# Clustered linear layer: count, gates and bias reordered, and the first value products of attention issued around the count

## The chip, the cores and the metric

The kernel runs on one NeuronCore of a Trainium2 chip. The metric is the device time of one execution in microseconds (us); a kernel's time is the median of several executions. Engines are called PE (TensorE), DVE (VectorE), ACT (ScalarE), POOL (GpSimd) and SP (SyncE).

## The reference, cut to what matters

Two layers over x of 16 x 64 tokens by 512 features. Layer 0 is a channel attention and then the clustered linear layer; layer 1 is a cross-attention with 32 query and 8 key/value heads, and a quantised SwiGLU. The change lies in the clustered linear layer and at the start of layer 1's attention.

```python
x = x + tanh(g_xattn[0]) * channel_attention(layernorm(x), ctx)
# clustered linear, on h = layernorm(x)
dots = softmax(h @ centroids.T / 0.1)          # 64 clusters
hits = dots > 0.01
query_sel = any(hits, axis=1)                  # per token
cluster_sel = any(hits, axis=0)                # per cluster, over ALL tokens
row_sel = cluster_sel[assignments]             # per output feature
dense = h @ weight.T + bias
x = x + tanh(g_ffn[0]) * where(query_sel[:, None] & row_sel[None, :], dense, 0)
# attention of layer 1 (masked softmax with rope), keys and values from ctx
k, v = ctx @ wk, ctx @ wv ;  q = layernorm(x) @ wq
x = x + tanh(g_xattn[1]) * attention(q, k, v) @ wo
x = x + tanh(g_ffn[1]) * swiglu_quantised(layernorm(x))
```

No token's output can be gated before the hits of all 1024 tokens are known, since `cluster_sel` runs over all of them.

## The kernel before, in words

Tokens lie in 8 tiles of 128 partitions (`TILES`), features in 4 chunks of 128 (`KC`). Each engine has its own program, and the programs are kept together by semaphores (`then_inc`, `wait_ge`). The order on each engine is written by hand. A large matmul is three matmuls of rounded parts: a high part `_hi` (made by ACT) and a rest `_lo` (made by DVE or POOL).

**`clustered_linear`** does this for tile `t`, with `p = t % 2` naming the buffers:
- DVE normalises `x_sb` into `xn` (`normalize`, two tiles ahead of the transposes' products); PE transposes it into the PSUM bank `TP[p]`; ACT rounds it (`split`, line 541) and DVE takes the rest (`split`, line 575).
- PE makes 24 matmuls (`products`, lines 660 and 662) into `DA[p]` (64 cluster columns and 224 dense ones) and `DB[p]` (288 dense ones). Tile t's products need the bank of tile t-2 free, so PE waits for that tile's exponential and its two bias additions (`s_exp`, `s_dense`).
- DVE takes the row maximum and scales it (lines 580, 583), adds the bias to both halves (585, 587), ACT takes the exponential (547). ACT's exponential also waits for the first bias addition, `act.wait_ge(s_dense, 2 * t + 1)`, and ACT's `split(t + 2)` stands behind the exponential.
- DVE (`hit`) inverts the sum, thresholds (594), adds the hits into `hit_sum` (597), takes the row's maximum (599) and multiplies by the gate (603).

After tile 7, PE multiplies `hit_sum` by ones into `CNT` (682), DVE turns the count into `selected` (636), and PE multiplies it by the one-hot assignments into the bank `ROW` (686). Then the block ends, and all engines meet before the next one.

**Weight pieces.** `raw` is a ring of 4 buffers. Eleven pieces (`NEXT`) of the first attention weights are loaded ahead; ACT rounds a piece (`round_piece`, 763) and POOL takes the rest (`split_piece`, 771), which counts in `s_piece`. Places 0 to 3 (two pieces of `wv`, two of `wq`) are rounded ahead of tile 0's exponential. Places 4 to 6 (`RING` to `FIRST`) are rounded by ACT behind the loop over tiles 0 to 5, ahead of the exponentials of tiles 6 and 7.

**`attention_and_swiglu`** begins in the next block. PE makes the value products of tiles 0 to 4 (12 matmuls of 256 columns each; `FIRST_V[t]` is half of the double bank `PB2`), with `key(0)` (12 matmuls of 512) in front of tile 2. DVE goes through `gate_linear(t)` (line 1484: dense times row gate times `ROW`), the row statistics of the updated rows (`rows`, behind POOL's `add_linear`), the rests of the values (`rest_v`, line 1432, behind ACT's rounding), and then normalises the tiles (`normalize_x`, line 1493), which PE transposes ahead of the first queries. From there on come ropes, scores and outputs.

Of the kernel before, what the change touches and what calls it, by code (L numbers as in the profile page):

```python
# [21 lines left out]
F32 = mybir.dt.float32  # L22
# [7 lines left out]
P = 128  # L30
# [444 lines left out]

def clustered_linear(nc, d, c):
# [12 lines left out]
    with ExitStack() as ctx:  # L489
# [20 lines left out]
        row_hit = sb("row_hit", [P, 2])  # L510
# [3 lines left out]
        TP = [bank("TP0_"), bank("TP1_")]  # L514
# [22 lines left out]
        @block.scalar  # L537
        def _(act):
            def split(t, p):
                act.wait_ge(s_t, t + 1)  # L540
                nc.scalar.activation(xt_hi[:, p, :, :], TP[p][:, :].rearrange("p (k t) -> p k t", k=KC),
                                     ACT.Copy).then_inc(s_hi, 1)

            def softmax(t, p):
                act.wait_ge(s_maxt, t + 1)
                act.wait_ge(s_dense, 2 * t + 1)
                nc.scalar.activation(e_cl[:, p, :], DA[p][:, 0:CLUSTERS], ACT.Exp,
                                     bias=nmax_t[:, p:p + 1], scale=INV_TEMPERATURE,
                                     accum_out=zsum[:, p:p + 1]).then_inc(s_exp, 1)

            split(0, 0)
            split(1, 1)
            for place in range(RING):
                round_piece(nc, act, c, 0, place, 0, *NEXT[place][:2])
            with act.Fori(0, TILES // 2 - 1) as i:
                for p in range(2):
                    softmax(2 * i + p, p)
                    split(2 * i + p + 2, p)
            for place in range(RING, FIRST):
                round_piece(nc, act, c, 0, place, 0, *NEXT[place][:2])  # L560
            for p in range(2):
                softmax(TILES - 2 + p, p)

        @block.vector
        def _(dve):
# [12 lines left out]
            def softmax_and_bias(t, p):  # L578
# [4 lines left out]
                nc.vector.tensor_scalar(nmax_t[:, p:p + 1], nmax[:, p:p + 1], INV_TEMPERATURE, None,  # L583
                                        ALU.mult).then_inc(s_maxt, 1)
                nc.vector.tensor_tensor(dense[:, t, 0:DENSE_A], DA[p][:, CLUSTERS:HALF],
                                        bias[:, 0:DENSE_A], ALU.add).then_inc(s_dense, 1)
                nc.vector.tensor_tensor(dense[:, t, DENSE_A:D], DB[p][:, 0:HALF],
                                        bias[:, DENSE_A:D], ALU.add).then_inc(s_dense, 1)

            def hit(t, p):  # L590
# [5 lines left out]
                dve.wait_ge(s_hit, t + 1)  # L596
                nc.vector.tensor_tensor(hit_sum[:, :], hit_sum[:, :], hits[:, p, :], ALU.add)\
                  .then_inc(s_sum, 1)
                nc.vector.tensor_reduce(row_hit[:, p:p + 1], hits[:, p, :], AX.X, ALU.max)\
                  .then_inc(s_row, 1)  # L600
                dve.wait_ge(s_row, t + 1)
                dve.wait_ge(s_sum, t + 1)
                nc.vector.tensor_tensor(row_gate[:, t, :], row_hit[:, p:p + 1], tg[:, 2:3], ALU.mult)\
                  .then_inc(s_gate, 1)
# [14 lines left out]
            def tile(t, p, ahead):  # L619
                softmax_and_bias(t, p)  # L620
# [3 lines left out]
                hit(t, p)  # L624

# [6 lines left out]
            for p in range(2):  # L632
                softmax_and_bias(TILES - 2 + p, p)
                hit(TILES - 2 + p, p)
            dve.wait_ge(s_cnt, 1)
            nc.vector.tensor_scalar(selected[:, :], CNT[0:CLUSTERS, 0:P], 0.0, None, ALU.is_gt)\
              .then_inc(s_sel, 1)

# [8 lines left out]
        def _(pe):  # L647
# [29 lines left out]
            for p in range(2):  # L677
# [3 lines left out]
            pe.wait_ge(s_sum, TILES)  # L681
            nc.tensor.matmul(CNT[0:CLUSTERS, 0:P], hit_sum[:, :], ones[:, :], start=True, stop=True)\
              .then_inc(s_cnt, 1)
            pe.wait_ge(s_sel, 1)
# [112 lines left out]
def attention_and_swiglu(nc, d, c, out):  # L797
# [13 lines left out]
    with ExitStack() as ctx:  # L811
# [34 lines left out]
        PB2 = ctx.enter_context(nc.psum_tensor("PB", [P, 2, 512], F32))  # L846
# [5 lines left out]
        s_q, s_k, s_v = sem("q_done"), sem("k_done"), sem("v_done")  # L852
# [942 lines left out]
        def _(pe):  # L1795
# [20 lines left out]
            def value(tile, bank=KV):  # L1816
                cols = slice(P * tile, P * tile + P)
                for k in range(KC):
                    mm = three(bank[:, 0:2 * DH], [x[:, k, cols] for x in (ctx_hi, ctx_lo)],
                               [w[:, k, :] for w in wv], k == 0, k == KC - 1)  # L1820
                mm.then_inc(s_v, 1)
# [322 lines left out]
def layer_0(nc, d, c, outer):  # L2144

    with ExitStack() as ctx:
# [14 lines left out]
        c["ROW"] = both["ROW"] = outer.enter_context(nc.psum_tensor("ROW", [P, 512], F32))  # L2161
        clustered_linear(nc, d, both)


def program(nc, d, out):
    with ExitStack() as ctx:
        def sb(name, shape, dt=F32):
# [26 lines left out]
            "s_piece": ctx.enter_context(nc.semaphore("pieces_split")),  # L2194
            "s_raw": [ctx.enter_context(nc.semaphore(f"raw{r}_loaded")) for r in range(RING)],
# [53 lines left out]
```

## Time and profile before

| what | us |
| --- | --- |
| median of 3 runs | 821.7 (820.88 to 821.91) |
| the profiled execution's own time | 820.62 |
| its span, first to last instruction | 818.8 |
| PE busy | 767.7 (94%) |
| DVE busy | 643.3 (79%) |
| POOL busy | 388.9 (47%) |
| ACT busy | 353.2 (43%) |

The span is what the trace covers; 1.8 us of the execution's own time lie outside it. Matmuls are pipelined, so a row of PE is longer than the distance from its start to the next one's. A group "xN" in a timeline is N instructions merged. The time in brackets at a row's end is how long the engine had stood idle, and what released it.

### The profile page before, as it was taken

Reading aid. Unit: us, or ns where it says so; the run is one execution under the profiler, and the core shown is the slowest. Engines: PE = TensorE matmul, PEld = TensorE weight load, DVE = VectorE, ACT = ScalarE, POOL = GpSimd, SP = SyncE. Lnnn points to the kernel's source line nnn. Section 1 sums busy time; section 2 is a strip of 40 time slices with the busy share of each in tenths; the row PEclk is TensorE's granted clock in tenths of the full one; section 3 lists DMA queues with packets and bytes.
Section 4 is the critical chain, followed back from the end, with each engine's and each line's share of the span. In section 5 each row is a group of like instructions: output and inputs, shape, how many; then the busy total and the mean of one; then the engine's idle time right before and its main releaser. Section 6 shows DMA issues by size and latency. Waiting matters only on the chain.

```text
span 818.8 us, 12666 instructions
## 1 busy us (share of the span) xinstructions
PE 767.7 (94%) x4276; PEld 607.9 (74%) x4276; DVE 643.3 (79%) x1216; ACT 353.2 (43%) x1072; POOL 388.9 (47%) x346
## 2 busy tenths in 40 slices
PE   2899998797989999999999999999999999999996
PEld 1566665696767878888887888888788888777875
DVE  5789888877988877777778777777777777868985
ACT  2687787221243333343333333343343334343765
POOL 2778777614264443233343423333343333477784
PEclk9999999997999999999999999999999999999999
DMA  8311030101021021010112101011110102120011
GB/s 261 113 26 51 26 109 0 40 1 52 1 64 52 26 65 39 27 31 22 52 29 63 40 26 40 26 39 52 41 41 24 40 26 91 30 54 1 1 38 67
DMA packets 37462, 37.44 MB, mean 46 GB/s; under 512 B 2912, under 2 KB 27232, under 8 KB 37408
## 3 DMA queue, kind: packets, MB, share of 16 engines
q1 hardware_dynamic: 35184, 32.81, 13.6%
q10 hardware_dynamic: 2224, 3.94, 1.5%
q8 instruction: 31, 0.51, 0.3%
q14 instruction: 23, 0.19, 0.1%
HBM read 34.64 MB, written 2.10 MB: 45 GB/s over the span
## 4 chain that ended last, share of the span: by engine, by line
PE 62%; DVE 7%; POOL 4%; issue 2%; ACT 1%; POOLq 0%; DVEq 0%; ACTq 0%
PE ROW L1798 6%; PE QB L1800 6%; PE SB L1918 6%; PE QB L1798 6%; PE QB L1799 6%; PE ROW L1799 6%; PE ROW L1800 6%; PE KV L1798 4%; PE PB L1891 4%; PE KV L1800 3%; PE KV L1799 3%; DVE rope_b L1413 2%; PE TB L1861 2%; POOL dense L978 1%; POOL wgu_raw L1052 1%
## 5 line engine op out<-in xcount | busy, mean ns | idle before, releaser
L978 POOL TENSOR_TENSOR dense<-rope_a,rope_b 128x512 f32<-128x512 f32 x62 | 79.2, 1278 | 163.7 <-DVE rope_b L1413 163.7
L1192 ACT ACTIVATE ot_hi<-PB 128x512 fp32r<-128x512 f32 x64 | 38.3, 598 | 199.1 <-PE PB L1891 199.1
L1181 ACT ACTIVATE e_sb<-masked,nmax 128x64 f32<-128x64 f32 x256 | 86.1, 337 | 56.8 <-DVE nmax L1444 56.4
L1798 PE MATMUL QB<-xT_hi,wq_lo 128*128 128x512 f32 x256 | 106.9, 417 | 0.0
L1798 PE MATMUL ROW<-wo_hi,ot_lo 128*128 128x512 f32 x256 | 102.3, 399 | 0.8 <-DVE ot_lo L1472 0.8
L1800 PE MATMUL QB<-xT_hi,wq_hi 128*128 128x512 f32 x256 | 101.7, 397 | 0.0
L1799 PE MATMUL ROW<-wo_lo,ot_hi 128*128 128x512 f32 x256 | 101.6, 397 | 0.0
L1799 PE MATMUL QB<-xT_lo,wq_hi 128*128 128x512 f32 x256 | 101.5, 397 | 0.0
L1800 PE MATMUL ROW<-wo_hi,ot_hi 128*128 128x512 f32 x256 | 101.1, 395 | 0.0
L1410 DVE TENSOR_TENSOR rope_a<-QB,rope 128x512 f32<-128x512 f32 x62 | 42.9, 691 | 74.1 <-PE QB L1800 72.0
L1413 DVE TENSOR_TENSOR rope_b<-QB,rope 64x512 f32<-64x512 f32 x124 | 85.4, 689 | 3.9
L1455 DVE TENSOR_TENSOR p_sb<-e_sb,rz 128x256 f32<-128x256 f32 x58 | 79.4, 1369 | 2.0
L372 POOL TENSOR_TENSOR prob<-prob,rz 128x512 f32<-128x512 f32 x64 | 67.9, 1068 | 21.7 <-DVE rz L266 20.6
L771 POOL TENSOR_TENSOR wq_lo<-raw,wq_hi 128x512 fp32r<-128x512 f32 x32 | 41.7, 1304 | 64.2 <-ACT wq_hi L763 64.2
L1918 PEld LDWEIGHTS SB<-k_rot,dense 128*128 128x128 f32 x512 | 63.5, 191 | 7.5 <-POOL dense L978 2.5
L1918 PE MATMUL SB<-k_rot,dense 128*128 128x64 f32 x512 | 66.3, 272 | 2.4 <-POOL dense L978 2.3
L192 ACT ACTIVATE prob<-RR,nmax 128x512 f32<-128x512 f32 x64 | 44.0, 688 | 32.4 <-DVE nmax L288 32.4
L1798 PEld LDWEIGHTS ROW<-wo_hi,ot_lo 128*128 128x128 f32 x256 | 48.4, 189 | 12.4 <-DVE ot_lo L1472 1.0
L1800 PEld LDWEIGHTS QB<-xT_hi,wq_hi 128*128 128x128 f32 x256 | 48.3, 189 | 11.8
L1800 PEld LDWEIGHTS ROW<-wo_hi,ot_hi 128*128 128x128 f32 x256 | 48.1, 188 | 11.7
L1799 PEld LDWEIGHTS ROW<-wo_lo,ot_hi 128*128 128x128 f32 x256 | 48.2, 188 | 10.9
L771 POOL TENSOR_TENSOR wo_lo<-raw,wo_hi 128x512 fp32r<-128x512 f32 x32 | 41.2, 1298 | 30.7 <-ACT wo_hi L763 30.7
(213 smaller groups left out, 1899.0 us busy)
## 6 DMA issues: line engine op xcount, KB each, us to landing
raw<-in_wq SPq DMA_DIRECT2D x32, 256.0 KB, 2.8
raw<-in_wo SPq DMA_DIRECT2D x32, 256.0 KB, 2.6
ctx_two<-in_ctx SPq DMA_DIRECT2D x16, 256.0 KB, 3.8
x_sb<-in_x SPq DMA_DIRECT2D x8, 256.0 KB, 7.5
ctx_raw<-in_ctxT ACTq DMA_DIRECT2D x1, 2048.0 KB, 12.1
raw<-in_wv SPq DMA_DIRECT2D x8, 256.0 KB, 2.7
raw<-in_wk SPq DMA_DIRECT2D x8, 256.0 KB, 2.9
out<-x_sb SPq DMA_DIRECT2D x8, 256.0 KB, 2.0
```

Source lines behind the costliest of these rows:

```text
L192: nc.scalar.activation(prob[:, u % 4, :], RR[u % 3][:, :], ACT.Exp, bias=nmax[:, u:u + 1], accum_out=zsum[:, u:u + 1])\
L372: nc.gpsimd.tensor_tensor(prob[:, u % 4, :], prob[:, u % 4, :], rz[:, u:u + 1].broadcast_to([P, D]), ALU.mult).then_inc(s_p, 1)
L771: nc.gpsimd.tensor_tensor(lo, raw_piece(c, place, kind), hi, ALU.subtract).then_inc(c["s_piece"], 1)
L978: nc.gpsimd.tensor_tensor(dst, a, b, ALU.add).then_inc(s_rot, 1)
L1181: nc.scalar.activation(e_sb[:, r, :], masked[:, r, :], ACT.Exp, bias=nmax[:, r:r + 1], accum_out=zsum[:, r:r + 1]).then_inc(s_exp, 1)
L1410: nc.vector.tensor_tensor(a, v, cos.broadcast_to([P, 8, S]), ALU.mult).then_inc(s_parts, 1)
L1413: nc.vector.tensor_tensor(b[other], v[rows], sin[rows].broadcast_to([S, 8, S]), ALU.mult)\
L1455: nc.vector.tensor_tensor(p_sb[:, N % 2, :, :], e_sb[:, :, :], rz[:, :].unsqueeze(2).broadcast_to([P, 4, S]), ALU.mult).then_inc(s_p, 1)
L1798: nc.tensor.matmul(out, lhs[1], rhs[0], start=first, stop=False)
L1799: nc.tensor.matmul(out, lhs[0], rhs[1], start=False, stop=False)
L1800: return nc.tensor.matmul(out, lhs[0], rhs[0], start=False, stop=last)
L1918: mm = nc.tensor.matmul(SB_[:, S * a:S * a + S], q, keys[:, S * b:S * b + S], start=True, stop=True)
```

## The change

- The bank pair `TP` of the clustered linear is now the double bank `PB2`, which the attention uses too.
- ACT: `split(t + 2)` stands ahead of `softmax(t)`; for tiles 6 and 7 the exponential no longer waits for the first bias addition; weight pieces 4 to 6 are rounded behind tile 1's exponential, and POOL's rests with them.
- DVE: `hit` no longer multiplies by the gate; one `tensor_scalar` makes all eight row gates at the end. The row's maximum comes ahead of the addition into `hit_sum`. In tile 6 and 7 the second bias half stands behind the maximum and the first half behind the hits (in tile 7 behind `selected`). Tile 7's hits are not added into `hit_sum`.
- PE: the count is two matmuls into the same bank, `hit_sum` of tiles 0 to 6 and then the hits of tile 7. Nine value products of tile 0 stand between them; tile 0's last three and tile 1's first three stand ahead of `ROW`. The attention's block begins with the other nine of tile 1 and the key.

```diff
+def value_products(nc, c, bank, tile, chunks):
+    cols = slice(P * tile, P * tile + P)
+    for k in chunks:
+        x, w = [a[:, k, cols] for a in (c["ctx_hi"], c["ctx_lo"])], [a[:, k, :] for a in c["wv"]]
+        nc.tensor.matmul(bank, x[1], w[0], start=(k == 0), stop=False)
+        nc.tensor.matmul(bank, x[0], w[1], start=False, stop=False)
+        mm = nc.tensor.matmul(bank, x[0], w[0], start=False, stop=(k == KC - 1))
+    return mm
...
-        TP = [bank("TP0_"), bank("TP1_")]
+        PB2 = c["PB2"]
+        TP = [PB2[:, p, :] for p in range(2)]
...
-            def softmax(t, p):
+            def softmax(t, p, biased=True):
                 act.wait_ge(s_maxt, t + 1)
-                act.wait_ge(s_dense, 2 * t + 1)
+                if biased:
+                    act.wait_ge(s_dense, 2 * t + 1)
...
-            with act.Fori(0, TILES // 2 - 1) as i:
-                for p in range(2):
-                    softmax(2 * i + p, p)
-                    split(2 * i + p + 2, p)
+            for p in range(2):
+                split(p + 2, p)
+                softmax(p, p)
             for place in range(RING, FIRST):
                 round_piece(nc, act, c, 0, place, 0, *NEXT[place][:2])
+            with act.Fori(1, TILES // 2 - 1) as i:
+                for p in range(2):
+                    split(2 * i + p + 2, p)
+                    softmax(2 * i + p, p)
             for p in range(2):
-                softmax(TILES - 2 + p, p)
+                softmax(TILES - 2 + p, p, False)
...
                 dve.wait_ge(s_hit, t + 1)
+                nc.vector.tensor_reduce(row_hit[:, t, :], hits[:, p, :], AX.X, ALU.max)\
+                  .then_inc(s_row, 1)
+
+            def add_hits(t, p):
                 nc.vector.tensor_tensor(hit_sum[:, :], hit_sum[:, :], hits[:, p, :], ALU.add)\
                   .then_inc(s_sum, 1)
-                nc.vector.tensor_reduce(row_hit[:, p:p + 1], hits[:, p, :], AX.X, ALU.max)\
-                  .then_inc(s_row, 1)
-                dve.wait_ge(s_row, t + 1)
                 dve.wait_ge(s_sum, t + 1)
-                nc.vector.tensor_tensor(row_gate[:, t, :], row_hit[:, p:p + 1], tg[:, 2:3], ALU.mult)\
-                  .then_inc(s_gate, 1)
...
-            for p in range(2):
-                softmax_and_bias(TILES - 2 + p, p)
-                hit(TILES - 2 + p, p)
+            maximum(TILES - 2, 0)
+            bias_b(TILES - 2, 0)
+            hit(TILES - 2, 0)
+            add_hits(TILES - 2, 0)
+            bias_a(TILES - 2, 0)
+            maximum(TILES - 1, 1)
+            bias_b(TILES - 1, 1)
+            hit(TILES - 1, 1)
             dve.wait_ge(s_cnt, 1)
             nc.vector.tensor_scalar(selected[:, :], CNT[0:CLUSTERS, 0:P], 0.0, None, ALU.is_gt)\
               .then_inc(s_sel, 1)
+            bias_a(TILES - 1, 1)
+            dve.wait_ge(s_row, TILES)
+            nc.vector.tensor_scalar(row_gate[:, :, 0], row_hit[:, :, 0], tg[:, 2:3], None, ALU.mult)\
+              .then_inc(s_gate, 1)
...
-            pe.wait_ge(s_sum, TILES)
-            nc.tensor.matmul(CNT[0:CLUSTERS, 0:P], hit_sum[:, :], ones[:, :], start=True, stop=True)\
+            pe.wait_ge(s_sum, TILES - 1)
+            nc.tensor.matmul(CNT[0:CLUSTERS, 0:P], hit_sum[:, :], ones[:, :], start=True, stop=False)
+            pe.wait_ge(c["s_piece"], 2)
+            first = [PB2[:, t, 0:2 * DH] for t in range(2)]
+            value_products(nc, c, first[0], 0, (0, 1, 2))
+            pe.wait_ge(s_hit, TILES)
+            nc.tensor.matmul(CNT[0:CLUSTERS, 0:P], hits[:, 1, :], ones[:, :], start=False, stop=True)\
               .then_inc(s_cnt, 1)
+            value_products(nc, c, first[0], 0, (3,)).then_inc(c["s_v"], 1)
+            value_products(nc, c, first[1], 1, (0,))
             pe.wait_ge(s_sel, 1)
             pe.wait_ge(s_oh, 1)
             nc.tensor.matmul(ROW[:, :], selected[:, :], one_hot[:, :], start=True, stop=True)
...
-            for tile in range(5):
-                if tile == 2:
-                    key(0)
-                if tile >= 2:
-                    pe.wait_ge(s_vlo, tile - 1)
+            value(1, FIRST_V[1], (1, 2, 3))
+            key(0)
+            for tile in (2, 3, 4):
+                pe.wait_ge(s_vlo, tile - 1)
                 value(tile, FIRST_V[tile])
```

## Rows read from the trace of the kernel before

**Rows 1.** The page of the profile: PE's busy time, and the chain's shares.

```profile
PE 767.7 (94%) x4276; PEld 607.9 (74%) x4276; DVE 643.3 (79%) x1216; ACT 353.2 (43%) x1072; POOL 388.9 (47%) x346
...
PE 62%; DVE 7%; POOL 4%; issue 2%; ACT 1%; POOLq 0%; DVEq 0%; ACTq 0%
```

**Rows 2.** Windows: PE, PEld, DVE, ACT, POOL busy, granted clock, DMA share, GB/s.

```profile
190.00:200.00 10.00, 9.70 (x37) 7.71 (x38) 6.68 (x14) 0.77 (x2) 5.76 (x5) 0.63 0.32 107
200.00:210.00 10.00, 8.35 (x58) 7.82 (x57) 9.26 (x18) 3.50 (x7) 5.50 (x5) 0.88 0.00 0
...
240.00:250.00 10.00, 7.67 (x36) 6.17 (x35) 8.90 (x15) 3.64 (x17) 4.84 (x4) 0.83 0.10 29
```

**Rows 3.** Timeline of VectorE: start us, duration us, engine, line, operation, tiles.

```profile
181.22 1.11 DVE L594 TENSOR_SCALAR hits<-e_cl,rz 128x64 f32<-128x64 f32 x1
182.37 1.24 DVE L597 TENSOR_TENSOR hit_sum<-hit_sum,hits 128x64 f32<-128x64 f32 x1
...
183.77 1.01 DVE L603 TENSOR_TENSOR row_gate<-row_hit,tg 128x1 f32<-128x1 f32 x1
184.71 0.21 DVE L580 TENSOR_REDUCE nmax<-DA 128x1 f32<-128x64 f32 x1
...
186.90 0.22 DVE L580 TENSOR_REDUCE nmax<-DA 128x1 f32<-128x64 f32 x1
...
187.22 0.38 DVE L585 TENSOR_TENSOR dense<-DA,bias 128x224 f32<-128x224 f32 x1
...
188.33 0.25 DVE L594 TENSOR_SCALAR hits<-e_cl,rz 128x64 f32<-128x64 f32 x1
188.62 0.22 DVE L597 TENSOR_TENSOR hit_sum<-hit_sum,hits 128x64 f32<-128x64 f32 x1
...
189.62 0.28 DVE L636 TENSOR_SCALAR selected<-CNT 64x128 f32<-64x128 f32 x1 [0.46 <-PE CNT L682]
```

**Rows 4.** Timeline of GpSimd, 148 to 215 us.

```profile
180.99 1.29 POOL L771 TENSOR_TENSOR wq_lo<-raw,wq_hi 128x512 fp32r<-128x512 f32 x1 [21.77 <-ACT wq_hi L763]
...
183.49 1.28 POOL L771 TENSOR_TENSOR wq_lo<-raw,wq_hi 128x512 fp32r<-128x512 f32 x1
193.15 5.01 POOL L972 TENSOR_TENSOR x_sb<-x_sb,dense 128x512 f32<-128x512 f32 x4 [8.38 <-DVE dense L1484]
```

**Rows 5.** Timeline of ScalarE: the last tile's exponential.

```profile
187.69 0.31 ACT L547 ACTIVATE e_cl<-DA,nmax_t 128x64 f32<-128x64 f32 x1 [1.78 <-DVE dense L585]
```

**Rows 6.** Timeline of TensorE, 183 to 205 us.

```profile
184.40 0.29 PE L662 MATMUL DB<-w_hi,xt_hi 128*128 128x288 f32 x1
188.90 0.69 PE L682 MATMUL CNT<-ones,hit_sum 128*64 128x128 f32 x2 [4.20 <-DVE hit_sum L597]
189.96 2.07 PE L686 MATMUL ROW<-one_hot,selected 64*128 64x512 f32 x2 [0.38 <-DVE selected L636]
192.33 0.55 PE L1798 MATMUL PB<-wv_hi,ctx_lo 128*128 128x256 f32 x1 [0.30 <-PEq L489]
...
200.35 0.28 PE L1799 MATMUL PB<-wv_lo,ctx_hi 128*128 128x256 f32 x1
200.47 0.28 PE L1800 MATMUL PB<-wv_hi,ctx_hi 128*128 128x256 f32 x1
```

**Rows 7.** Timeline of VectorE in the stage behind, 192 to 205 us.

```profile
195.68 0.42 DVE L1432 TENSOR_TENSOR v_lo<-PB,v_hi 128x256 fp32r<-128x256 f32 x1 [0.29 <-ACT v_hi L1198]
...
198.09 0.43 DVE L1432 TENSOR_TENSOR v_lo<-PB,v_hi 128x256 fp32r<-128x256 f32 x1 [0.52 <-ACT v_hi L1198]
...
202.29 0.42 DVE L1432 TENSOR_TENSOR v_lo<-PB,v_hi 128x256 fp32r<-128x256 f32 x1 [0.64 <-ACT v_hi L1198]
...
204.74 3.14 DVE L1493 TENSOR_SCALAR dense<-x_sb,mv,rstd 128x512 f32<-128x512 f32 x4
```

**Rows 8.** Timeline of TensorE inside the tile loop.

```profile
170.17 0.40 PE L660 MATMUL DA<-w_hi,xt_lo 128*128 128x288 f32 x1 [0.44 <-DVE xt_lo L575]
```

**Rows 9.** Timeline of VectorE at the first two tiles.

```profile
156.59 2.92 DVE L570 TENSOR_SCALAR xn<-x_sb,mv,rstd 128x512 f32<-128x512 f32 x2
```

More of the change, by code:

```diff
@@ L509, in clustered_linear @@
         ones = sb("ones", [P, P])
-        row_hit = sb("row_hit", [P, 2])
+        row_hit = sb("row_hit", [P, TILES, 1])
         assign_f = sb("assign_f", [CLUSTERS, D])
@@ L576, in split, with maximum @@
                                         xt_hi[:, p, :, :], ALU.subtract).then_inc(s_lo, 1)
-            def softmax_and_bias(t, p):
+            def maximum(t, p):
                 dve.wait_ge(s_mm, t + 1)
@@ L584, in softmax_and_bias, with bias_a, bias_b @@
                                         ALU.mult).then_inc(s_maxt, 1)
+            def bias_a(t, p):
                 nc.vector.tensor_tensor(dense[:, t, 0:DENSE_A], DA[p][:, CLUSTERS:HALF],
                                         bias[:, 0:DENSE_A], ALU.add).then_inc(s_dense, 1)
+            def bias_b(t, p):
                 nc.vector.tensor_tensor(dense[:, t, DENSE_A:D], DB[p][:, 0:HALF],
@@ L619, in tile @@
             def tile(t, p, ahead):
-                softmax_and_bias(t, p)
+                maximum(t, p)
+                bias_a(t, p)
+                bias_b(t, p)
                 split(t + 2, p)
@@ L624, in tile @@
                 hit(t, p)
+                add_hits(t, p)
             dve.wait_ge(s_rstd, 1)
@@ L845, in attention_and_swiglu @@
         KV, SB_, TB = (bank(n) for n in ("KV", "SB", "TB"))
-        PB2 = ctx.enter_context(nc.psum_tensor("PB", [P, 2, 512], F32))
+        PB2, s_v = c["PB2"], c["s_v"]
         PB = [PB2[:, b, 0:256] for b in range(2)]
@@ L851, in attention_and_swiglu @@
         s_xn, s_xt, s_xhi, s_xlo = sem("xn_ready"), sem("xn_transposed"), sem("xt_hi_ready"), sem("xt_lo_ready")
-        s_q, s_k, s_v = sem("q_done"), sem("k_done"), sem("v_done")
+        s_q, s_k = sem("q_done"), sem("k_done")
         s_s, s_t, s_pv, s_o = sem("scores_done"), sem("t_done"), sem("pv_done"), sem("o_done")
@@ L1814, in key, with value @@
                 mm.then_inc(s_k, 1)
[L1816 to L1821, printed above, removed]
+            def value(tile, bank=KV, chunks=range(KC)):
+                value_products(nc, c, bank[:, 0:2 * DH], tile, chunks).then_inc(s_v, 1)
             def transpose_x(t):
@@ L2161, in layer_0 @@
         c["ROW"] = both["ROW"] = outer.enter_context(nc.psum_tensor("ROW", [P, 512], F32))
+        c["PB2"] = both["PB2"] = outer.enter_context(nc.psum_tensor("PB", [P, 2, 512], F32))
         clustered_linear(nc, d, both)
@@ L2194, in program @@
             "s_piece": ctx.enter_context(nc.semaphore("pieces_split")),
+            "s_v": ctx.enter_context(nc.semaphore("values_done")),
             "s_raw": [ctx.enter_context(nc.semaphore(f"raw{r}_loaded")) for r in range(RING)],
```

## The prediction

> **What bounds the kernel now.** The page comes first: PE is busy 94% of the span, and it holds 62% of the chain that ended last, VectorE 7% [rows 1]. So the kernel is PE's, and a change off PE matters only where PE stands still or runs slowly. The windows show where: from 190 to 200 us the granted clock averages 0.63 of full speed, from 200 to 210 us 0.88, from 240 to 250 us 0.83 [rows 2]; nearly all other windows of 10 us from 160 us on have 1.00. The first of these is the end of the clustered linear layer and the start of the attention. There the timelines have to be read by hand, because two stretches chained by small instructions lie in it.
>
> In the tail of the linear layer, PE starts its last product at 184.40 (ends 184.69), the count at 188.90, `ROW` at 189.96 and the first value product of the next block at 192.33 [rows 6]. That is 7.64 us for work of less than 3 us. VectorE is what PE waits for: it takes tile 6's maximum only at 184.71 and tile 7's at 186.90 [rows 3], though tile 6's products had been finished some 3.3 us before tile 7's. The reason stands just ahead. Three of its small instructions take 1.11, 1.24 and 1.01 us; tile 7's hits and sum take 0.25 and 0.22 [rows 3]. At that time GpSimd works on three weight pieces of 1.29 us each, from 180.99 to 184.77 [rows 4], and the slow ones end when a piece ends: 182.33 against 182.28, 184.78 against 184.77. So VectorE stood behind GpSimd for about 0.86 + 1.02 + 0.85 = 2.7 us.
>
> Behind the tail, from 192.33 us, VectorE sets the pace until the first scores (in the chain, its instructions alternate there with a few of GpSimd), and PE's values are beside it. VectorE waits for three of ScalarE's rounded values, 0.29, 0.52 and 0.64 us [rows 7], and normalises from 204.74 on.
>
> **The change part by part.** I count from E, the end of tile 7's products.
>
> *Pieces in tile 1, and the order on ScalarE.* GpSimd is free at the tail. Without its 2.7 us VectorE would reach tile 6's maximum at 182.0 and, with the 2.19 us that tile 6 took (184.71 to 186.90), be done at 184.2, before E. So tile 7's maximum starts at about E + 0.06 and not E + 2.21: 2.15 us. ScalarE's `split` ahead of the exponential also spares VectorE its wait of 0.6 us for it in each tile, and `hit` is one instruction and one wait shorter. PE had at least one stall of 0.44 us on `xt_lo` in the loop [rows 8]; I take 0.3 us for E itself (between 0, if the moved pieces eat it up, and 0.7).
>
> *What the pieces cost in tile 1.* They would run from about 164.5 to 168.4 us, when VectorE has the normalisation of tile 5, tile 1's hits and their sum. I work it out as at the old place: each waits for the end of a piece, so VectorE reaches tile 2's maximum at 167.2 to 168.5 us (before 167.7), and the rest for tile 4 is ready near 169.9; PE was released at 170.17 for it [rows 8]. It then has a loop that is 0.6 to 0.8 us shorter per tile to catch up in before tile 6. The cover is this slack; gone, it costs up to the 2.7 us again.
> By the Trainium skill (SBUF — State Buffer, "Who interferes with whom"), `tensor_scalar` between SBUF operands and `tensor_tensor` with both inputs in SBUF contend with GpSimd, the second to come is blocked for the whole instruction, and a reduction never is. The trace agrees: the blocked three are of these forms [rows 3, 4]. By that rule the scaling of tile 2's maximum is blocked too, the later of my two times above; that would take some 0.3 us from the sum.
>
> *Bias behind the hits.* Before, the exponential started at 187.69 [rows 5], behind the bias half of 187.22 to 187.60 [rows 3]. Now it can start when that half did, plus a signal: 0.3 us saved. From the maximum to the end of the hits was 188.58 - 186.90 = 1.68; now 1.38, ending at E + 1.44. The removed sum of tile 7 saves 0.26 more on the path (188.58 to 188.84).
>
> *The count.* Its first half and nine value products lie in PE's wait: 0.2 + 9 x 0.12 (the distance from 200.35 to 200.47 [rows 6]) = 1.3 us, ready as the hits are. The second half starts at E + 1.5. From the count to `selected` were 0.72 us (188.90 to 189.62), at half clock. PE now comes from continuous work, so I take full clock and 0.5 us: E + 2.0. `selected` takes 0.28 [rows 3], so `ROW` could start at E + 2.35; the six value products behind the count end at 1.5 + 0.2 + 6 x 0.12 = E + 2.4. `ROW` took 2.07 us at half clock [rows 6], 1.05 at full: E + 3.45. The bias half and the single row gate, 0.38 and about 0.2 us, are under `ROW`. The next block began 0.30 us behind [rows 6]: E + 3.75. Before it was E + 7.64. Gain 3.9 us, and 0.3 for E: 4.2.
>
> *The attention's start.* Fifteen of 24 value products are done, and the clock is warm: value 1 is ready 1.1 us into the block and value 2 at 5.3 us, so the three waits of 0.29 + 0.52 + 0.64 = 1.45 us go [rows 7]. What is late next is GpSimd's addition, 1.25 us a tile (5.01 for 4 [rows 4]), which I put at 0.35; and the four normalisations, 3.14 us beside such additions [rows 7], overlap them 0.5 us longer, 0.3. Net 0.8 (between 0 and 1.4).
>
> Sum: 4.2 + 0.8 = 5.0 us, on PE's path until the end, as PE is busy in nearly every later window. The profiled execution took 820.62 us (span 818.8 and 1.8 around it) and would take 815.6. It lies 1.1 us below the median 821.7, which gives 816.7 us.
>
> **The rivals.**
>
> *The moved pieces bite.* The three pieces cost PE 1.3 to 2.7 us between tile 1 and 4: for it, two normalisations beside pieces took 2.92 us at tile 1 already [rows 9]; against it, the worked times above, with products being PE's for 3.6 us a tile. 821.7 - 5.0 + 2.0 = 818.7 us. Chance 0.12.
>
> *The clock stays or falls low in the tail.* Then the count costs 0.2 more, `ROW` 1.0, and the values and the key behind it some 2 us of which half is under VectorE's work: 818.5 us. For it: the clock was 0.63 here [rows 2]. Against it: that fall lay behind 4.2 us of idle PE, and now the idle pieces are a few tenths. By the Trainium skill (TensorE: Matmul & The Clock Gate, "What's actually happening"), the clock goes by windows that run freely, so the point of change differs between executions of one kernel; no single trace shows that. Chance 0.12.
>
> *It is hidden.* The next block starts earlier, but something not tied to it (a piece of the ring, an engine that comes late to the meeting of the blocks) holds it or the first scores at the old time. Against it, the loads behind it are issued when the block begins, and the seven pieces before are finished by 169 us. 821 us. Chance 0.07.
>
> *Slower.* Value 4 must wait for VectorE's rest of value 2, near 9 us into the block, and the transposes for the normalisations near 12. PE idles there about 3.5 us, the clock falls as it did before 210 us (0.88 [rows 2]), and here it would stay low through values 5 and 6 and the four first queries: 24 x 0.12 and 48 x 0.24 = 14.4 us more, of which about half lies under VectorE's ropes. Then 816.7 + 7.5 = 824 us. It decides once the low stretch costs PE over 5 us beyond its slack, some 35 to 40 of the 72 matmuls; before, the clock was back at full by 211 us. Chance 0.05.
>
> **How the numbers follow.** Forecast 0.62, with its own range 815.2 to 818.2 from the bounds on E, on the attention's start and on the stretch at 240 us, where the low clock of some 3 us may move or go. The named rivals hold 0.36, and a gain above 6.5 us the remaining 0.02. For 8 in 10 I go from 814.8 to 819.8. About 0.2%, 1.6 us, is what a measurement of this kernel can tell: faster 0.88 (forecast, first two rivals, the larger gain), same 0.07, slower 0.05.
>
> **What would show it.** VectorE's hits and sums of tile 5 at 0.25 us; tile 7's maximum less than 0.2 us behind the last product; under 2 us from there to the second count; `ROW` near 1.05 us at granted clock 1.00; the next block about 3.8 us behind the last product and near 188.1 us; the first normalisation of the attention near 199.4 us, and from 250 us on the same distances as before. Slow instructions of VectorE should stand at 164 to 168 us. The prediction is wrong if a PE stall of over 1 us shows at tiles 3 to 5, if `ROW` is still 2 us, or if the attention's first scores start less than 4 us earlier.

## The result and the profile after

The median fell from 820.88 us (17 runs, 817.08 to 822.92) to 816.52 us (17 runs, 813.08 to 818.43); the ratio is 0.995 with a 95% interval of 0.9936 to 0.9964. A second series of the same kernel gave 816.39 us and 0.9934 (0.9915 to 0.9953). The forecast was 816.7 us.

Single executions of one kernel lie up to 6 us apart, so the whole time is a coarse measure for parts of the change. The distances inside the stage are much finer. I take them from tile 0's maximum (the first `nmax<-DA` row of VectorE) and use six of them throughout:

```
from tile 0's maximum, us            E      tile 7's  next   first      second     first
                                            maximum   block  norm. four norm. four scores
before                               25.26  27.47     32.90  45.31      55.32      71.87
before, second profile               25.27  27.48     32.91  45.45      55.45      72.01
after                                24.13  24.17     28.38  39.02      49.97      66.51
after, second profile                24.13  24.17     28.38  39.02      49.98      66.54
```

E is the end of tile 7's products, "next block" the first work of VectorE in the attention block, "norm. four" the first and the second group of four normalisations (`dense<-x_sb,mv,rstd`) there, and the scores are PE's first `SB<-k_rot,dense`. Two profiles of one kernel agree within 0.15 us. The change is worth 5.4 us up to the first scores. From those scores to the last update of `x_sb` the kernels take 584.4 (before) and 585.0 us (after); over all fourteen profiles this rest lies between 583.3 and 585.5 us, so the difference of 0.6 us is not told apart from scatter.

The page of the kernel after, with the lines that answer to [rows 1]:

```profile
PE 768.4 (94%) x4278; PEld 608.6 (75%) x4278; DVE 640.9 (78%) x1208; ACT 353.8 (43%) x1072; POOL 388.8 (48%) x346
...
PE 61%; DVE 7%; POOL 5%; issue 2%; ACT 1%; POOLq 0%; DVEq 0%; ACTq 0%
```

Windows of 10 us of the kernel after; the granted clock is the column behind the five engines:

```profile
190.00:200.00 10.00, 8.02 (x54) 7.36 (x55) 9.50 (x20) 1.54 (x4) 7.73 (x7) 1.00 0.36 107
200.00:210.00 10.00, 8.10 (x48) 7.36 (x47) 9.73 (x18) 3.16 (x6) 3.51 (x3) 0.66 0.00 0
...
240.00:250.00 10.00, 9.23 (x43) 7.33 (x43) 8.81 (x14) 2.87 (x12) 4.25 (x4) 0.83 0.11 37
```

The dip at the end of the linear layer is gone (1.00 from 190 to 200 us, 0.63 before [rows 2]) and a deeper one stands at 200 to 210 us (0.66 for 0.88). The timeline of VectorE in the tail of the kernel after:

```profile
184.41 0.21 DVE L621 TENSOR_TENSOR hit_sum<-hit_sum,hits 128x64 f32<-128x64 f32 x1
...
186.03 0.22 DVE L596 TENSOR_REDUCE nmax<-DA 128x1 f32<-128x64 f32 x1 [0.98 <-PE DB L693]
...
187.11 0.25 DVE L614 TENSOR_SCALAR hits<-e_cl,rz 128x64 f32<-128x64 f32 x1
...
188.02 0.28 DVE L663 TENSOR_SCALAR selected<-CNT 64x128 f32<-64x128 f32 x1 [0.40 <-PE CNT L718]
```

The sum of tile 6 takes 0.21 us, tile 7's maximum follows 0.04 us behind the last product, and its hits come 1.08 us later; the answer to [rows 3]. TensorE in the same stretch, against [rows 6]:

```profile
185.92 0.43 PE L713 MATMUL CNT<-ones,hit_sum 128*64 128x128 f32 x2
...
187.54 0.43 PE L718 MATMUL CNT<-ones,hits 128*64 128x128 f32 x2
...
188.82 1.12 PE L724 MATMUL ROW<-one_hot,selected 64*128 64x512 f32 x2
190.24 0.36 PE L481 MATMUL PB<-wv_hi,ctx_lo 128*128 128x256 f32 x1 [0.30 <-PEq L500]
```

The last product ends at 185.99. PE is busy through the count; the count's halves take 0.43 us for 0.69, and `ROW` 1.12 for 2.07. From the last product to the next block are 4.25 us, 7.64 before.

Where VectorE meets GpSimd now, first GpSimd's rows of the kernel after:

```profile
166.88 1.47 POOL L809 TENSOR_TENSOR wq_lo<-raw,wq_hi 128x512 fp32r<-128x512 f32 x1 [5.22 <-ACT wq_hi L801]
168.31 1.28 POOL L809 TENSOR_TENSOR wk_lo<-raw,wk_hi 128x512 fp32r<-128x512 f32 x1
169.56 1.27 POOL L809 TENSOR_TENSOR wq_lo<-raw,wq_hi 128x512 fp32r<-128x512 f32 x1
...
199.59 3.91 POOL L1010 TENSOR_TENSOR x_sb<-x_sb,dense 128x512 f32<-128x512 f32 x3
```

and VectorE's, in tile 1 and at the attention's first normalisations:

```profile
167.31 1.10 DVE L614 TENSOR_SCALAR hits<-e_cl,rz 128x64 f32<-128x64 f32 x1
...
168.69 0.99 DVE L621 TENSOR_TENSOR hit_sum<-hit_sum,hits 128x64 f32<-128x64 f32 x1
...
170.54 0.15 DVE L599 TENSOR_SCALAR nmax_t<-nmax 128x1 f32<-128x1 f32 x1
...
200.88 3.83 DVE L1531 TENSOR_SCALAR dense<-x_sb,mv,rstd 128x512 f32<-128x512 f32 x4
```

The hits and the sum of tile 1 take 1.10 and 0.99 us. They stood at 0.25 and 0.22 where no piece ran [rows 3]. The four normalisations take 3.83 us beside GpSimd's additions (3.14 before [rows 7]).

Both profiles of the kernel after begin the linear layer late, at 153.19 us against 150.78. That is not the change: of the 2.4 us, 1.7 arise in the last outputs of the channel attention, 16 matmuls that no edit touches. They took 5.35 us in these and in the second profile of before (whose linear layer began at 152.88), and 3.65 in the first profile of before and in the ten other profiles below. The granted clock from 145 to 150 us is 0.66 in the three executions and 1.00 in the eleven. The other 0.7 us lie further ahead still (these matmuls start at 145.38 us in after and 144.66 in before), where the code is the same too; their cause was not looked for.

### The profile page after: what moved, and what is told of

Same layout as the page of the kernel before. It is cut to its first block, busy times and chain, and to the rows that moved or that the text cites. A ratio compares the mean times of both kernels' runs of the same rounds, so it can differ in the third digit from the quotient of the medians.

```text
span 816.6 us, 12648 instructions
## 1 busy us (share of the span) xinstructions
PE 768.4 (94%) x4278; PEld 608.6 (75%) x4278; DVE 640.9 (78%) x1208; ACT 353.8 (43%) x1072; POOL 388.8 (48%) x346
## 3 DMA queue, kind: packets, MB, share of 16 engines
HBM read 34.64 MB, written 2.10 MB: 45 GB/s over the span
## 4 chain that ended last, share of the span: by engine, by line
PE 61%; DVE 7%; POOL 5%; issue 2%; ACT 1%; POOLq 0%; DVEq 0%; ACTq 0%
PE ROW L1836 6%; PE QB L1836 6%; PE SB L1951 6%; PE QB L1837 6%; PE QB L1838 6%; PE ROW L1837 6%; PE ROW L1838 6%; PE PB L1924 4%; DVE rope_b L1451 2%; PE KV L481 2%; PE KV L1836 2%; PE TB L1894 2%; PE KV L1838 1%; PE KV L1837 1%; PE KV L482 1%
```

## The experiments

The distances of all runs, from the profiles (the time is the median of each series, the ratio that to the kernel before in the same series):

```
                          E     max 7  block  norm 1 norm 2 scores  median  ratio (95%)
pieces alone              29.15 29.19  34.64  46.31  56.41  72.97   822.56  1.0016 (0.9998-1.0033)
ScalarE's order alone     23.92 23.96  28.20  39.73  49.98  66.53   816.86  0.9944 (0.9921-0.9967)
after, pieces back        23.98 24.02  28.22  38.86  49.57  66.12   816.58  0.9944 (0.9929-0.9959)
after, exponential first  28.89 28.93  33.13  43.78  54.47  71.03   820.41  0.9981 (0.9964-0.9997)
after, values back        24.13 24.17  27.79  39.37  49.56  66.12   815.05  0.9937 (0.9915-0.9959)
after, bias ahead         24.13 24.24  28.68  39.31  50.27  66.83   815.82  0.9939 (0.9915-0.9963)
after, three values fewer 24.13 24.17  28.02  38.67  49.38  65.93   813.74  0.9910 (0.9886-0.9935)
 + late additions         24.13 24.17  28.02  38.65  47.43  63.98   814.24  0.9918 (0.9894-0.9942)
order + late additions    23.94 23.98  28.22  39.89  48.67  65.23   814.67  0.9910 (0.9888-0.9932)
 pieces back, three fewer,
 late additions           23.93 23.97  27.82  38.45  47.23  63.79   815.19  0.9930 (0.9911-0.9949)
```

**The pieces alone.** Before, with pieces 4 to 6 rounded behind tile 1's exponential:

```diff
-            with act.Fori(0, TILES // 2 - 1) as i:
+            for p in range(2):
+                softmax(p, p)
+                split(p + 2, p)
+            for place in range(RING, FIRST):
+                round_piece(nc, act, c, 0, place, 0, *NEXT[place][:2])
+            with act.Fori(1, TILES // 2 - 1) as i:
                 for p in range(2):
                     softmax(2 * i + p, p)
                     split(2 * i + p + 2, p)
-            for place in range(RING, FIRST):
-                round_piece(nc, act, c, 0, place, 0, *NEXT[place][:2])
```

> The kernel before, with only one edit: weight pieces 4 to 6 are rounded behind tile 1's exponential instead of behind the loop. D1 is the distance from the linear layer's first normalisation to the first value product of the attention block (41.55 us before, 37.05 after). Theory A (the tail was held by VectorE standing behind GpSimd): tile 7's maximum comes 2.15 us earlier, D1 is 39.4 us or a little less, and the kernel is 2 us faster than before. Theory B (the stall is only moved to tile 1, and what helped was PE's value work in the tail): D1 stays within 0.5 us of 41.55, and the time within 0.5 us of before.

D1 is 43.30 us and lies outside the ranges of both theories: the next block begins 1.74 us later than before, and the time does not fall. VectorE and TensorE of this run at tile 1:

```profile
163.39 1.53 DVE L573 TENSOR_SCALAR xn<-x_sb,mv,rstd 128x512 f32 x1
...
165.03 1.08 DVE L597 TENSOR_SCALAR hits<-e_cl,rz 128x64 f32<-128x64 f32 x1
166.15 1.23 DVE L600 TENSOR_TENSOR hit_sum<-hit_sum,hits 128x64 f32<-128x64 f32 x1
...
168.23 0.22 DVE L583 TENSOR_REDUCE nmax<-DA 128x1 f32<-128x64 f32 x1 [0.42 <-issue]
```

```profile
170.70 0.40 PE L663 MATMUL DA<-w_hi,xt_lo 128*128 128x288 f32 x1 [3.27 <-DVE xt_lo L578]
```

These three instructions of VectorE stand behind a piece each (0.54, 0.26 and 0.23 us in the kernel before), and tile 2's maximum comes 11.23 us behind tile 0's instead of 8.27. In the old order VectorE has no slack, so PE runs dry for 3.27 us on `xt_lo`. The tail itself did get 2.15 us shorter (from E to the next block 5.49 for 7.64), as expected; the loop lost 3.89 (E 29.15 for 25.26). Theory A holds for the tail and fails for the whole; of theory B, "only moved" is what happened, and more than that was lost; its other half, that the value products are what helped, this run can't show.

**The pieces back in the tail.** The reverse edit on the kernel after:

```diff
-            for place in range(RING, FIRST):
-                round_piece(nc, act, c, 0, place, 0, *NEXT[place][:2])
             with act.Fori(1, TILES // 2 - 1) as i:
                 for p in range(2):
                     split(2 * i + p + 2, p)
                     softmax(2 * i + p, p)
+            for place in range(RING, FIRST):
+                round_piece(nc, act, c, 0, place, 0, *NEXT[place][:2])
```

> The kernel after, with only the weight pieces 4 to 6 put back behind ScalarE's loop. Theory A: the hits and sums of tiles 5 and 6 stand behind GpSimd again, but VectorE is now ahead of PE by about 1 us per tile, so a part is under the last products: D1 is 37.5 to 39.5 us, and the kernel 0.5 to 2.5 us slower than after. Theory B: D1 within 0.3 us of 37.05 and no slower than after.

Not slower than after: E comes 0.15 us and the next block 0.16 us earlier. (D1 is 37.68 us, which lies in theory A's range, but 0.79 of it is the way from the first normalisation to tile 0's maximum, 9.46 us here for 8.67, ahead of anything the edit touches.) In the new order VectorE stands behind GpSimd in the tail too (1.07 and 1.03 us in the rows below), but waits for PE anyway in front of its maxima, and the delay goes into that wait.

```profile
178.37 0.22 DVE L596 TENSOR_REDUCE nmax<-DA 128x1 f32<-128x64 f32 x1 [1.20 <-PE DB L693]
...
180.59 1.07 DVE L621 TENSOR_TENSOR hit_sum<-hit_sum,hits 128x64 f32<-128x64 f32 x1
182.00 0.23 DVE L596 TENSOR_REDUCE nmax<-DA 128x1 f32<-128x64 f32 x1 [0.34 <-PE DB L693]
...
183.09 1.03 DVE L614 TENSOR_SCALAR hits<-e_cl,rz 128x64 f32<-128x64 f32 x1
...
185.13 0.23 DVE L596 TENSOR_REDUCE nmax<-DA 128x1 f32<-128x64 f32 x1 [0.20 <-PE DB L693]
```

Theory A fails here: with the rest of the change in place, the place of the pieces is worth nothing.

**ScalarE's order taken back, and alone.** The edit on the kernel after, and the mirrored one on the kernel before (where the pieces stay behind the loop):

```diff
             for p in range(2):
-                split(p + 2, p)
                 softmax(p, p)
+                split(p + 2, p)
...
                 for p in range(2):
-                    split(2 * i + p + 2, p)
                     softmax(2 * i + p, p)
+                    split(2 * i + p + 2, p)
```

> The kernel after, with only ScalarE's order put back in the loop: the exponential of tile t ahead of the rounding of tile t+2 (the weight pieces stay behind tile 1). D3 is the distance from tile 0's maximum to the attention block's first work (32.90 us before, 28.38 after, 34.64 with the pieces alone moved). Theory D (what pays is the shorter loop of VectorE, which no longer waits 0.6 us per tile for ScalarE's rounding; the moved pieces pay nothing by themselves): the stall of about 3 us at tile 1 is no longer caught up, tile 7's products end 2 to 3.5 us later than in after, D3 is 30.5 to 32 us and the kernel 2 to 3.5 us slower than after. Rival (the order is worth nothing, bias and count carry the gain): D3 within 0.5 us of 28.38.

> The kernel before, with only ScalarE's order changed: the rounding of tile t+2 ahead of the exponential of tile t; the weight pieces stay behind the loop, count, bias and gates as before. Theory D: VectorE comes to the tail ahead of PE, most of the 2.7 us behind GpSimd lie under the last products, tile 7's maximum follows its products within 1 us; D3 is 29.5 to 31 us (32.90 before), and the time 2 to 3.4 us under before. Rival: the pieces in the tail hold VectorE all the same, D3 at least 32 us.

Both go theory D's way, and both beyond its ranges. Without the order the next block is 4.75 us later than in after and E 4.76; the order alone, on the kernel before, reaches 28.20, 49.98 and 66.53 where the whole change has 28.38, 49.97 and 66.51. The waits of 150 to 192 us show what it removes (columns: total us, times, longest). The kernel before:

```profile
ACT e_cl L547 <- DVE dense L585: 25.2, 8, 5.1
...
DVE xt_lo L575 <- ACT xt_hi L541: 4.5, 7, 0.9
```

The run with the exponential first:

```profile
DVE xt_lo L591 <- ACT xt_hi L553: 4.6, 7, 0.9
...
PE DA L691 <- DVE xt_lo L591: 4.0, 2, 3.0
```

and the run with the order alone, where only VectorE's and PE's waits of tile 0 are left:

```profile
ACT xt_hi L541 <- PE TP_ L654: 23.9, 7, 8.4
...
PE DA L663 <- DVE xt_lo L578: 1.0, 1, 1.0
DVE xt_lo L578 <- ACT xt_hi L541: 0.9, 1, 0.9
```

In the old order ScalarE's rounding stands behind an exponential that waits for VectorE's bias addition, so each tile VectorE adds the bias and then stands still until ScalarE has come through both. In the new order ScalarE waits for PE's transposes and has rounded before VectorE asks.

The tail of the run with the order alone, on VectorE and on PE:

```profile
181.73 0.22 DVE L583 TENSOR_REDUCE nmax<-DA 128x1 f32<-128x64 f32 x1
```

```profile
183.74 0.43 PE L685 MATMUL CNT<-ones,hit_sum 128*64 128x128 f32 x2 [2.05 <-DVE hit_sum L600]
184.55 1.12 PE L689 MATMUL ROW<-one_hot,selected 64*128 64x512 f32 x2 [0.38 <-DVE selected L639]
185.97 0.55 PE L1801 MATMUL PB<-wv_hi,ctx_lo 128*128 128x256 f32 x1 [0.30 <-PEq L489]
```

Its 4.70 us up to the next block are 1.34 us at E, 2.17 us at tile 7's maximum (0.04 us behind E for 2.21), and 1.19 us from there on, because the count and `ROW` take 0.43 and 1.12 us instead of 0.69 and 2.07. So about a quarter of it is the granted clock.

The other parts are worth something where the order is missing. Bias, hits, count and values on top of the moved pieces, in the old order (the run with the exponential first against the one with the pieces alone), bring the next block from 34.64 to 33.13 us and the scores from 72.97 to 71.03. On top of the new order, with the pieces in the tail, they bring 28.20 to 28.22 and 66.53 to 66.12. They and the order gain largely the same microseconds. Those parts were not run on the kernel before without the order and without the moved pieces.

**The value products back in the attention block.**

```diff
-            value_products(nc, c, first[0], 0, (0, 1, 2))
...
-            value_products(nc, c, first[0], 0, (3,)).then_inc(c["s_v"], 1)
-            value_products(nc, c, first[1], 1, (0,))
...
-            value(1, FIRST_V[1], (1, 2, 3))
+            value(0, FIRST_V[0])
+            value(1, FIRST_V[1])
```

> The kernel after, with the 15 value products put back behind the block's end; the count stays in two halves. Theory A (they use idle PE, keep the clock and spare VectorE's waits): the last product to the next block takes 3.3 us with the clock at 1.00 and up to 4.9 us with it fallen, the stage to the attention's first normalisation is 0.8 to 1.5 us longer than the 10.64 of after; the whole is 1 to 3 us slower than after. Theory C (the value products only fill idle time of PE behind VectorE, and the rest of the chain does not care): within 0.4 us of after in both stages.

Stage by stage neither theory holds. From the last product to the next block are 3.66 us, 0.59 less than in after, and theory C gave 0.4 either way; the stage behind is 0.94 us longer, which is in theory A's range. Theory A's forecast for the whole, 1 to 3 us slower, fails: the first scores come 0.39 us earlier without them. TensorE of this run:

```profile
180.86 0.43 PE L713 MATMUL CNT<-ones,hit_sum 128*64 128x128 f32 x2
182.36 0.43 PE L715 MATMUL CNT<-ones,hits 128*64 128x128 f32 x2 [1.07 <-DVE hits L614]
183.17 1.12 PE L719 MATMUL ROW<-one_hot,selected 64*128 64x512 f32 x2 [0.37 <-DVE selected L663]
184.59 0.55 PE L481 MATMUL PB<-wv_hi,ctx_lo 128*128 128x256 f32 x1 [0.30 <-PEq L500]
```

`ROW` starts 0.34 us behind `selected` and takes 1.12 us, half of the 2.07 of [rows 6], although PE stood idle 1.07 and 0.37 us. So the head start of the values buys 0.94 us in the attention's first stage (11.58 against 10.64), of which 0.59 is lost ahead of `ROW`, and the rest and a little more at the normalisations. The clock does fall in this run, but behind `ROW`: the first value product takes 0.55 us where it took 0.36 in after, and the granted clock from 180 to 190 us is 0.83, against 1.00 in after. In after it falls later, from 200 to 210 us.

**The bias ahead of the hits again.** In tiles 6 and 7 both bias halves stand behind the maximum and the exponential behind the first.

```diff
-            maximum(TILES - 2, 0)
-            bias_b(TILES - 2, 0)
-            hit(TILES - 2, 0)
-            add_hits(TILES - 2, 0)
-            bias_a(TILES - 2, 0)
-            maximum(TILES - 1, 1)
-            bias_b(TILES - 1, 1)
-            hit(TILES - 1, 1)
+            for p in range(2):
+                maximum(TILES - 2 + p, p)
+                bias_a(TILES - 2 + p, p)
+                bias_b(TILES - 2 + p, p)
+                hit(TILES - 2 + p, p)
+                if p == 0:
+                    add_hits(TILES - 2, 0)
...
-                softmax(TILES - 2 + p, p, False)
+                softmax(TILES - 2 + p, p)
```

> The kernel after, with the bias additions of tiles 6 and 7 ahead of the hits as before and the exponential behind the first of them; tile 7's hits still go straight into the count. Theory A: tile 7's hits come 0.3 us later (1.68 instead of 1.33 us from its maximum), D1 is 37.35 us, and the time 0.3 us above after, which is hardly measurable. Rival: the nine value products end as late as the hits, so that nothing is lost: D1 37.05.

From tile 0's maximum the next block is 0.30 us later, and this stays until the scores (66.83 for 66.51). In the whole time it is lost, as expected.

**Three value products fewer, and GpSimd's additions late.** The first run takes tile 1's first three products out from ahead of `ROW`:

```diff
-            value_products(nc, c, first[1], 1, (0,))
...
-            value(1, FIRST_V[1], (1, 2, 3))
+            value(1, FIRST_V[1])
```

The second adds

```diff
+            pool.wait_ge(s_xn, 4)
             for t in range(5, TILES):
                 add_linear(t)
```

> The kernel after, with tile 1's first three value products back in the attention block, so that three and not six stand between the count and ROW. If ROW waited for PE and not for `selected` (it began 0.80 us behind selected's start in after, 0.34 in before), D3 is 0.4 us shorter, 28.0 us, and the time 0.2 to 0.4 us under after. Rival: `selected` sets it, D3 28.38.

> The kernel after, with three value products fewer ahead of ROW as in the run beside it, and GpSimd waiting for the attention's first four normalisations before it makes its last three additions of the linear layer. Theory E (the normalisations took 3.83 us in after only because each stands behind one of these additions; alone four take 1.92): the four take 1.92 us, from the first of them to the second four are 9.0 us instead of 10.95, and the kernel is 1.8 to 2.3 us faster than after. Rival: the additions come too late for the rows of tiles 5 to 7, the second four normalisations stay at 10.5 us or more behind the first, and nothing is gained.

The first gains its 0.36 us. Its median is 2.8 us under after's first series, of which the profiles show 0.6 up to the scores and 1.7 behind them (583.3 us to the last update for 585.0), where no edit works; so most of it is scatter. In the second, the rows of GpSimd and VectorE show what the normalisations had waited for:

```profile
194.93 1.02 POOL L63 TENSOR_TENSOR rstd<-veps,mhalf 128x4 f32<-128x4 f32 x1 [1.18 <-DVE veps L57]
199.19 3.81 POOL L1009 TENSOR_TENSOR x_sb<-x_sb,dense 128x512 f32<-128x512 f32 x3 [3.24 <-DVE dense L1531]
```

```profile
197.20 1.91 DVE L1531 TENSOR_SCALAR dense<-x_sb,mv,rstd 128x512 f32<-128x512 f32 x4
...
205.98 1.92 DVE L1531 TENSOR_SCALAR dense<-x_sb,mv,rstd 128x512 f32<-128x512 f32 x4 [1.20 <-POOL rstd L63]
```

Four take 1.91 us instead of 3.83, the second four begin 8.78 us behind the first instead of 10.71 without the wait (10.95 in after), and the first scores come 1.95 us earlier. Theory E holds for the distances. In whole times these 1.95 us don't show: 814.24 us with the wait, 813.74 without it, in the same series; in the profiles 0.8 us are lost again behind the scores (584.1 us to the last update for 583.3).

**Together.** The order and the late additions on the kernel before; and the change with both extras and the pieces back.

> The kernel before with two edits only: ScalarE's order in the loop (rounding of tile t+2 ahead of the exponential), and GpSimd's wait for the attention's first four normalisations. Theory D and E together: D3 28.2 us as with the order alone, from the first to the second four normalisations 9.0 us instead of 10.25, the time 1.2 us under that of the order alone and 1 us under the full change. Rival: without the trimmed count and values the order alone is only by chance as good, D3 above 29 us here.

> The kernel after with the weight pieces back behind the loop, three value products fewer ahead of ROW, and GpSimd's last three additions behind the normalisations. If the gains add up: D3 27.9 us (28.38 - 0.36 - 0.15), the first scores 63.6 to 64.0 us behind tile 0's maximum (66.51 in after), and the time 2 to 3 us under after. Rival: the pieces in the tail now cost what they did not before, D3 28.4 or more.

Both are the edits shown above, put together. Distances as expected in both (28.22, and 8.78 between the normalisations; 27.82, and 63.79 to the scores). The shortest way to the scores is the last one's, 63.79, 2.7 us under after. In whole times the last one is 1.2 us under after in the same series (815.19 for 816.39), where 2 to 3 were expected. The four improved kernels lie at 813.7 to 815.2 us with ratios of 0.991 to 0.993, whose intervals overlap each other and that of after's second series; that they beat the kernel before is clear, their order among themselves is not.

**The kernels of before and after once more.**

> The kernel after once more, for a second profile and for times beside the two runs above. If the late start of the linear layer in the first profile of after (its first normalisation at 153.19 us, 150.78 in before) was the granted clock of that execution and no effect of the change, it will differ between these profiles by 1 to 3 us with D3 unchanged at 28.4. If it is an effect of the change, it is near 153.2 again.

> The kernel before once more, for a second profile: D3 at 32.9 us within 0.3 or, with the clock falling at another point, within 1 us; the start of the linear layer between 148 and 154 us.

The distances repeat (28.38 and 32.91). The start of the linear layer was 153.79 and 152.88 us. By the first of the two texts alone, a start near 153.2 us again spoke for an effect of the change. The second profile of before, as late, speaks against it, and so do the 3.65 us of these matmuls in the four runs whose code up to there is that of after (values back, bias ahead, three values fewer, and with late additions). The late start goes with executions in which the clock was low at 145 to 150 us, with the kernel before as with the one after.

## Why the prediction was right in size, and wrong in its cause

- **E, the end of tile 7's products: 0.3 us forecast, 1.13 measured.** This term was mis-sized, and with the next it is where the cause was misread. I took the 0.6 us that VectorE no longer waits for ScalarE's `split` as a small extra; it is the change. I had one stall of PE, at tile 4 [rows 8], and the rows of before show three: PE starts the products 1.04, 0.58 and 0.68 us behind the start of the transposes ahead of them, where 0.36 is the distance in the other tiles, 1.2 us in all. In the old order VectorE needs 3.9 us per tile beside PE's 3.6 and stands still 4.5 us in all for `xt_hi`, seven times (the list of waits of before; 0.9 us, once, with the order alone); in the new one it is ahead of PE from tile 5 on (tile 5's, 6's and 7's maxima wait 0.17, 1.19 and 0.98 us for the products), and with the pieces still in the tail tile 2's maximum waits for PE already (0.60 us).

```profile
169.13 0.60 PE L651 MATMUL TP_<-ident,xn 128*128 128x128 f32 x4
...
173.47 0.60 PE L651 MATMUL TP_<-ident,xn 128*128 128x128 f32 x4
174.05 0.40 PE L660 MATMUL DA<-w_hi,xt_lo 128*128 128x288 f32 x1
...
177.36 0.60 PE L651 MATMUL TP_<-ident,xn 128*128 128x128 f32 x4
178.04 0.38 PE L660 MATMUL DA<-w_hi,xt_lo 128*128 128x288 f32 x1
```

- **The 2.15 us for the moved pieces is the step that failed.** That tile 7's maximum follows its products at once was right (0.04 us). The cause was not: with the order alone, and the pieces still in the tail, it follows as closely, 0.04 us; with the pieces alone moved the tail gives just these 2.15 us and the loop takes 3.89. At tile 7's maximum the two do the same thing, and once the order is in place the moved pieces are worth nothing (they cost 0.15 us). My reading of the 2.7 us behind GpSimd was right as a fact, and wrong as a price, since slack ahead of the tail covers it as well.
- **The cost of the pieces in tile 1: 0.15 us where I had none, and so little only by the slack.** Tile 2's maximum came at 8.42 us behind tile 0's, before at 8.27, and PE started tile 4's products 0.53 us behind its transposes instead of 0.36; with the pieces back, E is 0.15 us earlier. The rival "the moved pieces bite" is true of the kernel without the new order (PE idle 3.27 us), at more than the 1.3 to 2.7 us that I had priced.
- **Bias and sum: 0.3 us each on the path.** The bias measured 0.30, in its own run and in the tail (1.33 us from maximum to the hits' end for 1.68). What dropping the last sum gives was not run alone.
- **The count: right in kind, 0.5 us too short.** From E to the next block I had 3.75 us, it is 4.25. The second count starts at E + 1.55 (1.5), but the six value products behind it end late: `ROW` starts at E + 2.83, not 2.4, while `selected` was there at 2.03 + 0.28. The run with three fewer gets 0.36 back, the one with none 0.59.
- **The clock: `ROW` at full clock, as forecast, and not because of the value products.** Without them PE idles 1.07 and 0.37 us and `ROW` takes the same 1.12 us. What lowers it is only half told: before, PE had waited 4.2 us; with the order alone, with and without the late additions, it waited 2.05 us and `ROW` took 1.12 us; with the pieces alone it also waited 2.05 us, and `ROW` took 2.07. With the order alone the low clock came as well, only behind `ROW` (the first value product took 0.55 us). Why it came ahead of the count in one of these runs and behind `ROW` in the others stays open.
- **The attention's start: 0.8 net forecast, 0.84 measured,** but as 1.77 gained and 0.93 lost. The three waits are gone as said. The loss is the four normalisations behind GpSimd (3.83 for 3.14 us) and the clock: PE waits 1.74 and 1.60 us there, and the transposes take 1.11 us for 0.66 at the low clock. The slower rival named this place; it cost VectorE one wait of 0.16 us for a rounded tile, not 7.5 us.
- **The Trainium skill's rule on the shared interfaces** (SBUF — State Buffer, "Who interferes with whom") held for hits, sums and normalisations, and not for what I drew from it: tile 2's one-column scaling took 0.15 us from 170.54 while a piece ran from 169.56 to 170.83. That section ties the two-port modes of `tensor_scalar` to further conditions on the operands, which I had left out.
- **Two sums are off.** The terms of the clock rival add up to 2.2 us and 818.9 us, not 818.5. And a value product at the low clock stands 0.21 us from the next for 0.12 at the full one (192.68 and 192.89 us in before), so it costs 0.09 us more and not the 0.12 of the slower rival. Neither moves the forecast.

So the number came out partly by luck. Up to the first scores the sum gave 5.0 us and 5.36 were measured, with the gain at E 0.8 us too small, the way from E to the next block 0.5 too short, and a price of 2.15 us given to an edit that did not earn it. The medians of 17 runs fell by 4.4 us. The forecast of 816.7 us started from 821.7, a median of 3 runs, while the 17 have 820.88: with the same 5.0 us it would have been 815.9, and its 0.2 us from the measured 816.52 says more of this start than of the sum.

## What to carry to other kernels

When two engines alternate in a loop, look at which of them is a few tenths per tile behind: an order that takes one wait out of it makes slack, and slack absorbs stalls at both ends of the loop that look like separate faults. Test a change of several edits by each one alone and by each one taken back; here three of four parts looked needed in the trace, and the fourth, taken for a small extra, reached alone what all four did. That does not make the others worthless where it is missing: in the old order, with the pieces moved, bias, count and values still gained 1.5 us up to the next block. Where whole times scatter by several us, distances between two fixed instructions in the profiles repeat to 0.15 us and decide what the times cannot. They show only the stage they span, and a gain there is a gain of the kernel only as far as the whole times bear it out.

## What the runs showed of the hardware

- An instruction of VectorE with two SBUF inputs or a wide SBUF-to-SBUF `tensor_scalar` ends with the GpSimd instruction that was running when it came: sums of 0.22 us became 0.99 to 1.24, hits of 0.25 became 1.03 to 1.11, a normalisation of 0.48 us (1.91 for four) became 0.96 (3.83). GpSimd's own instruction grew from 1.28 to 1.47 us where a normalisation of VectorE was under way when it came (166.88 us in after).
- A one-column `tensor_scalar` was not held (0.15 us), a one-column `tensor_tensor` with two SBUF inputs was (1.01 us [rows 3]).
- The same 16 matmuls took 3.65 us in eleven profiles (granted clock 1.00 from 145 to 150 us) and 5.35 in three (0.66), with identical code ahead of them: the granted clock of an execution can fall in a stretch where it does not in the next, which is 1.7 us of the scatter of the whole times.
